# A hybrid layer on one core: the state-space stage with its last convolution tap in the projection's bank, its step size as one fp32r product, and its jobs in another order

## The chip, the cores and the metric

The kernel runs on one core of a Trainium2 chip. The core has a matrix engine (TensorE, PE in the profile; its weight loads are shown apart as PEld), a vector engine (VectorE, DVE), a scalar engine (ScalarE, ACT), a programmable engine (GpSimd, POOL), and a queue engine (SyncE, SP) that issues the transfers. Each engine runs its own instruction list in order, and they wait for one another through semaphores. SBUF is the on-chip memory, PSUM the eight banks into which PE writes. The metric is the device time of one execution in microseconds (us); less is better.

## The reference

The input is x with shape (16, 512, 256): 16 rows of 512 tokens with 256 channels, in fp32. Four residual layers follow one another, each on a layer norm: a state-space layer, a mixture of 8 experts, causal attention, and the same mixture again. Only the first one is touched here:

```python
xz = x @ in_proj_w + in_proj_b
xc, z = jnp.split(xz, 2, axis=-1)                 # 512 channels each
xc = silu(causal depthwise conv of 4 taps over the tokens (xc) + conv_b)
dBu = xc @ x_proj_w + x_proj_b
delta_s, B, u = jnp.split(dBu, [16, 32], axis=-1) # 16, 16, 512 wide
delta = softplus(delta_s @ dt_proj_w + dt_proj_b)
A = -jnp.arange(1, 17)
h[t] = exp(delta[t] * A) * h[t-1] + delta[t] * B[t] * u[t]   # 512 x 16 states
y = h.sum(-1) + u * D
y = y * silu(z)
out = x + (y @ out_proj_w + out_proj_b)
```

## The kernel before

The state-space stage is `mamba_phase`, which fills the span from the start to about 1750 us; the experts and the attention follow in phases of their own and are not touched. Channels lie on the 128 partitions (four groups of 128, numbered m or dt), tokens along the free axis (512). A row's 16 states times four groups are worked off as 32 steps (`STEPS`), two states a step. Step s of a row is: ACT makes `exp(-n*delta)` for two states into the PSUM tile `da` (two activations, `decay_step`, L686), POOL multiplies `du` with the broadcast B rows into `dbu` (`input_step`, L599), DVE runs one scan over 1024 elements into `hs` (`scan_step`, L738), and PE adds the two states of all tokens, transposing, into the bank `yT` (`sum_step`, eight transposes, L838).

How far the engines can run apart is set by their buffers. `da` has two, so decay s waits for scan s-2. `dbu` and `hs` have four (`DEEP`), so dbu s waits for scan s-4, and scan s waits for sum s-4 of PE.

Three rows are in flight. A turn of 32 steps runs `main` work of row turn-1 (the steps), `first` work of row turn (norm, projection, convolution, step size), and `late` work of row turn-2 (output projection, residual, routing). There are 18 turns; turns 3 to 14 run in a hardware loop of two turns a pass. What stands where is written by hand: each engine has a `one_turn` with lines of the form `if s == 9 and first:`, and behind each step's own instruction comes what is listed for that s.

The extra work goes through three PSUM banks, `ring`. `RING_JOBS` is the order in which jobs take them; a job's bank is its index modulo 3, and PE waits (`job_bank`) until the job three places before it has been read. `MM_JOBS`, `ACT_JOBS` and `DVE_JOBS` are the orders in which the jobs' semaphores are raised. The jobs are: T0, T1 the transposed row; I0 to I3 and Z0 to Z3 the two halves of the input projection (`in_proj`, L792); S the 16 step-size inputs and the 16 B values (`x_proj_small`, L808); DA0 to DA3 the step size (`dt_proj`, L822); U0 to U3 the inputs u (`x_proj`, L815); G0 to G3 the summed y turned back (`turn_back`, L846); O0, O1 the output projection (`out_proj`, L855 for the bias, L857); RT0, RT1, RL, RP the routing.

The steps of the code that the change touches: 

- The convolution (`conv_input`, `conv_taps`). ACT copies the projection from its bank to `xc` (L621), and writes the last tap, scaled and with its bias, to `last_tap` (L624). PE overwrites the bank with three shifted products with diagonal matrices (L800), and adds `last_tap` with a fourth product with the identity (L801).
- The step size. ACT adds the bias and writes S to `db`, 48 partitions (`delta_b`, L656). PE multiplies `db[0:32]` with `w_dt` in fp32 (L822). SP stores `db[32:48]` to memory, from where it is spread to all partitions as `bb`. ACT then takes |v| and relu(v) (`step_size`, L660, L661), exp and log (`exp_part`, `log_part`, L666, L670), with a table load on either side of the log, and POOL adds the two parts (`softplus`, L605).
- The output bias, an fp32 product over 32 partitions of which one is used (L855), one for each of four token groups.
- `skip_input` (L676) writes u*D into `uD`, `step_input` (L728) makes `du`, `gate` (L746) makes y*silu(z), `residual` (L751) adds the row, `route_apply` and `prompt_apply` are the norms' four activations (L190).

## Time and profile before

| | us |
|---|---|
| median of 3 runs | 3327.88 (3322.89 to 3331.84) |
| the profiled execution | 3320.98 |
| its span, first to last instruction | 3319.2 |
| state-space stage, about | 0 to 1750 |
| two turns in the loop (678.36 to 893.47) | 215.1 |

The profile comes from one execution. Busy time of an engine counts its computing instructions; the ends of PE's instructions are modelled, so that the distance between the starts of two of them says more than the length of one. An fp32 product of PE leaves two records. "Idle before" is the time in which an engine stood still ahead of an instruction, with what ended the wait.

### The profile page before, as it was taken

To read this page: it belongs to the slowest core of one execution; us is meant where nothing else is said; L and a number is where in the kernel's file an instruction comes from. 1 tells how busy PE (TensorE), PEld (TensorE's weight loads), DVE (VectorE), ACT (ScalarE), POOL (GpSimd) and SP (SyncE) were. 2 spreads that over 40 slices of the span, in tenths; PEclk is the share of its full clock that TensorE was granted. 3 is DMA by queue.
4 is the path that set the end of the run, shared out by engine and by line. 5 is a ranking of instruction groups with operands and counts; after the bars stand their busy time and mean duration, and the time that the engine had idled before them with its cause. 6 is when DMAs were issued, how large, how long until landed. Compare 5 with 4: busy or idle time off the path is not lost. (4 is left out here: it accounts for less than half of the span.)

```text
span 3319.2 us, 54728 instructions
## 1 busy us (share of the span) xinstructions
PE 2964.6 (89%) x17184; PEld 2291.2 (69%) x17184; DVE 2348.4 (71%) x4213; ACT 1764.5 (53%) x3332; POOL 2189.2 (66%) x1403
## 2 busy tenths in 40 slices
PE   6899989989999899899974999999699995999998
PEld 2566555655656556565653999999577774999998
DVE  2888888888888888888883665665466664566564
ACT  3756666566756666566642554544233333444453
POOL 2878887888888888888884555554134434555554
PEclk8999999999999999999986999999899997999999
DMA  4221211121101211121124454452222223445442
GB/s 116 99 98 66 79 69 50 41 80 71 72 24 72 80 64 54 41 79 69 57 98 146 113 127 92 123 120 53 85 83 85 95 79 106 105 112 125 93 124 47
DMA packets 192656, 281.60 MB, mean 85 GB/s; under 512 B 35941, under 2 KB 164618, under 8 KB 184260
## 3 DMA queue, kind: packets, MB, share of 16 engines
q1 hardware_dynamic: 157124, 236.31, 21.3%
q0 software_dynamic: 35328, 42.76, 7.1%
q8 instruction: 105, 1.72, 0.2%
q14 instruction: 99, 0.81, 0.1%
HBM read 197.28 MB, written 94.72 MB: 88 GB/s over the span
## 5 line engine op out<-in xcount | busy, mean ns | idle before, releaser
L599 POOL TENSOR_TENSOR dbu<-du,bb 128x1024 f32<-128x1024 f32 x512 | 1199.9, 2362 | 152.2 <-DVE hs L738 147.4
L738 DVE TENSOR_TENSOR_SCAN hs<-da,dbu 128x1024 f32<-128x1024 f32 x512 | 1150.8, 2279 | 103.4 <-ACT da L686 36.1
L686 ACT ACTIVATE da<-delta 128x512 f32<-128x512 f32 x1024 | 570.1, 595 | 291.8 <-DVE hs L738 277.5
L838 PEld LDWEIGHTS yT<-ident,hs 128*128 128x128 f32 x4096 | 483.4, 146 | 168.3 <-issue 133.6
L838 PE MATMUL yT<-ident,hs 128*128 128x128 f32 x4096 | 540.5, 281 | 22.4 <-DVE hs L738 22.4
L1304 POOL TENSOR_TENSOR ffn_w_lo<-ffn_w,ffn_w_hi 128x512 fp32r<-128x512 f32 x256 | 344.6, 1373 | 170.0 <-ACT ffn_w_hi L1299 165.8
L1350 PE MATMUL ffn_hbank<-ffn_rowsT_hi,ffn_w_hi 128*128 128x320 f32 x1024 | 339.0, 331 | 43.0 <-DVE ffn_hT_lo L1372 40.8
L1384 PE MATMUL ffn_ybank<-ffn_w_hi,ffn_hT_hi 128*128 128x256 f32 x1280 | 364.4, 285 | 0.7 <-DVE ffn_hT_lo L1372 0.7
L1386 PE MATMUL ffn_ybank<-ffn_w_hi,ffn_hT_lo 128*128 128x256 f32 x1280 | 359.3, 281 | 0.0
L1385 PE MATMUL ffn_ybank<-ffn_w_lo,ffn_hT_hi 128*128 128x256 f32 x1280 | 359.0, 280 | 0.0
L1351 PE MATMUL ffn_hbank<-ffn_rowsT_lo,ffn_w_hi 128*128 128x320 f32 x1024 | 318.9, 311 | 0.0
L1352 PE MATMUL ffn_hbank<-ffn_rowsT_hi,ffn_w_lo 128*128 128x320 f32 x1024 | 318.8, 311 | 0.0
L1370 DVE TENSOR_SCALAR ffn_hbank<-ffn_hbank,ffn_b 128x320 f32<-128x320 f32 x512 | 281.8, 550 | 48.0 <-ACT ffn_hT_hi L1361 46.7
L1361 ACT ACTIVATE ffn_hT_hi<-ffn_hbank,ffn_b 128x320 fp32r<-128x320 f32 x512 | 263.1, 526 | 89.6 <-PE ffn_hbank L1352 87.5
L1401 DVE SCALAR_TENSOR_TENSOR ffn_y<-ffn_b,ffn_part,ffn_y 128x256 f32<-128x256 f32 x160 | 77.6, 485 | 312.7 <-ACT ffn_y L1395 312.7
L387 POOL DMA_INDIRECT slots<-a_r_xn,a_r_send x128 | 128.4, 1003 | 246.7 <-DVE a_r_send L377 211.1
L792 PE MATMUL ring<-xnT,w_in 128*128 128x512 f32 x512 | 252.8, 629 | 27.5 <-ACT uD L676 23.9
L1395 ACT ACTIVATE ffn_y<-ffn_ybank,ffn_part 128x256 f32<-128x256 f32 x160 | 76.0, 475 | 358.7 <-PE ffn_ybank L1386 185.2
L1372 DVE TENSOR_TENSOR ffn_hT_lo<-ffn_hbank,ffn_hT_hi 128x320 fp32r<-128x320 f32 x512 | 251.6, 491 | 17.6
L815 PE MATMUL ring<-hx,w_x 128*128 128x512 f32 x512 | 251.1, 626 | 1.2 <-ACT delta L661 1.2
L1384 PEld LDWEIGHTS ffn_ybank<-ffn_w_hi,ffn_hT_hi 128*128 128x128 f32 x1280 | 241.5, 189 | 1.1 <-DVE ffn_hT_lo L1372 1.1
L1385 PEld LDWEIGHTS ffn_ybank<-ffn_w_lo,ffn_hT_hi 128*128 128x128 f32 x1280 | 241.6, 189 | 0.0
(233 smaller groups left out, 5349.0 us busy)
## 6 DMA issues: line engine op xcount, KB each, us to landing
bb<-b_rows SPq DMA_DIRECT2D x64, 1024.0 KB, 4.5
ffn_w<-L_ffn_W SPq DMA_DIRECT2D x64, 1024.0 KB, 10.1
slots<-empty SPq DMA_DIRECT2D x40, 530.0 KB, 7.2
ffn_rows<-slots SPq DMA_DIRECT2D x32, 662.5 KB, 5.0
a_x<-x_after_mamba SPq DMA_DIRECT2D x32, 512.0 KB
xt<-L_attn_a_x SPq DMA_DIRECT2D x16, 512.0 KB
x<-L_attn_a_x SPq DMA_DIRECT2D x16, 512.0 KB, 4.0
x_after_mamba<-x SPq DMA_DIRECT2D x16, 512.0 KB, 3.0
```

Of the source, the lines that this page charges most:

```text
L599: pool.tensor_tensor(dbu[:, s % DEEP], du[:, dt, :].unsqueeze(1).to_broadcast([P, SN, T]), bb[:, q * SN:(q + 1) * SN, :], ALU.mult).then_i ...
L686: ins = act.activation(da[:, s % 2, i, :], delta[:, par, dt, :], ACT.Exp, scale=-float(q * SN + i + 1))
L738: dve.tensor_tensor_scan(flat[0], flat[1], flat[2], 0.0, ALU.mult, ALU.add).then_inc(scanned.sem, 1)
L838: mm = pe.matmul(yT[:, j * P:(j + 1) * P], hs[:, s % DEEP, i, j * P:(j + 1) * P], k.ident[:], start=False, stop=(q == QS - 1 and i == SN - ...
L1304: pool.tensor_tensor(low, full, high.bitcast(F32), ALU.subtract).then_inc(w_lo.sem, 1)
L1350: pe.matmul(hbank[:, job % 4, 0:HW], w1_hi[:, par, c, ws], rowsT_hi[:, c, rs], start=(c == 0), stop=False)
L1351: pe.matmul(hbank[:, job % 4, 0:HW], w1_hi[:, par, c, ws], rowsT_lo[:, c, rs], start=False, stop=False)
L1352: mm = pe.matmul(hbank[:, job % 4, 0:HW], w1_lo[:, par, c, ws], rowsT_hi[:, c, rs], start=False, stop=(c == NC - 1))
L1370: dve.tensor_scalar(bank, bank, b1[:, par, m:m + 1], 0.0, ALU.add, ALU.max).then_inc(h_full.sem, 1)
L1384: pe.matmul(bank, hT_hi[:, m, rs], w2_hi[:, par, m, :], start=(m == 0), stop=False)
L1385: pe.matmul(bank, hT_hi[:, m, rs], w2_lo[:, par, m, :], start=False, stop=False)
L1386: mm = pe.matmul(bank, hT_lo[:, m, rs], w2_hi[:, par, m, :], start=False, stop=(m == NH - 1))
```

## The change

Three pieces of arithmetic and one of order.

1. **Last tap.** ACT writes the scaled last tap back into the projection's own bank, and the three diagonal products add to it. `last_tap` and the identity product are gone.
2. **Step size.** `w_x` carries the 16 step-size columns three times, so that S has 112 rows: three copies and B. ACT writes 96 rows as fp32r (rounded) to `db` and the B rows to a tile of their own, `b_turn`; DVE replaces the middle copy by its rounding error (`delta_low`). `w_dt` holds rounded weights, rounded weights, and the weights' rounding error. One fp32r product over 96 partitions is then high*high + low*high + high*low. S is raised by DVE now, no longer by ACT, and `store_b` follows the second of ACT's two writes.
3. **Output bias** as three bf16 parts on three partitions, one bf16 product. The parts of weights and bias are made once, by DVE in turns 0 and 1 (`stage_weights`, `stage_bias`), from `x1` as a scratch tile; SP loads 21 instead of 11 constants.
4. **Order.** Jobs and the engines' lines are moved.

```diff
-XW = DI + 48
+XW = DI + 112
...
-RING_JOBS = ("G3", "Z0", "O0", "U2", "T0", "T1", "U3", "I0", "I1", "G0", "O1", "Z1", "I2", "I3", "RT0", "S", "DA0",
-             "DA1", "RT1", "DA2", "DA3", "G1", "RL", "U0", "Z2", "U1", "G2", "RP", "Z3", "-")
+RING_JOBS = ("G3", "Z0", "U2", "T0", "T1", "O0", "U3", "I0", "I1", "O1", "G0", "Z1", "I2", "I3", "RT0", "S", "DA0",
+             "DA1", "RT1", "DA2", "G1", "DA3", "U0", "RL", "Z2", "U1", "G2", "RP", "Z3", "-")
...
             act.activation(xc[:, m, DC - 1:], bank, ACT.Identity, bias=b_in[:, m:m + 1])
-            if has_first(turn - 1) or m >= 2:
-                act.wait_ge(conv_mm.sem, conv_mm.at(turn, m - 1))
-            act.activation(last_tap[:, m % 2, :], bank, ACT.Identity, bias=b_tap[:, m:m + 1],
+            act.activation(bank, bank, ACT.Identity, bias=b_tap[:, m:m + 1],
                            scale=w_conv[:, m, DC - 1:DC]).then_inc(conv_in.sem, 1)
...
-            act.activation(db[:], bank_of("S")[0:48, :], ACT.Identity, bias=b_db[:]).then_inc(act_took.sem, 1)
+            act.activation(db[0:96, :], bank_of("S")[0:96, :], ACT.Identity, bias=b_db[0:96, :]).then_inc(s_split.sem, 1)
+            act.activation(b_turn[96:112, :], bank_of("S")[96:112, :], ACT.Identity,
+                           bias=b_db[96:112, :]).then_inc(s_split.sem, 1)
...
+        def delta_low(dve, turn):
+
+            dve.wait_ge(s_split.sem, s_split.at(turn, 2))
+            dve.scalar_tensor_tensor(db[32:64, :], bank_of("S")[32:64, :], b_db[32:64, :], db[32:64, :].bitcast(F32),
+                                     ALU.add, ALU.subtract).then_inc(dve_took.sem, 1)
...
             for tap in range(DC - 1):
-                pe.matmul(bank, w_diag[:, m, tap, :], xc[:, m, tap:tap + T], start=(tap == 0), stop=False)
-            mm = pe.matmul(bank, k.ident[:], last_tap[:, m % 2, :], start=False, stop=True)
+                mm = pe.matmul(bank, w_diag[:, m, tap, :], xc[:, m, tap:tap + T], start=False,
+                               stop=(tap == DC - 2), skip_group_check=True)
...
-            pe.matmul(bank, w_dt[:, m * P:(m + 1) * P], db[0:32, :], start=True, stop=True).then_inc(ring_mm.sem, 1)
+            pe.matmul(bank, w_dt[:, m * P:(m + 1) * P], db[0:96, :], start=True, stop=True).then_inc(ring_mm.sem, 1)
...
+                        if s == 15 and late:
+                            route_apply(act, turn, turn - 2)
...
+                        if s == 20 and first:
+                            delta_low(dve, turn)
```

What moves, at three places. PE, steps 15 to 20 of turn 2: S (L808), uD (L833), the step-size products (L822), G1 (L846), the routing's turn (L865) and score (L873), the sums (L838). Before:

```order
L808 MATMUL ring<-hx,w_x 48x512 x2
L833 MATMUL yT<-ident,uD 128x128 x4
L838 MATMUL yT<-ident,hs 128x128 x8
L822 MATMUL ring<-db,w_dt 128x512
L838 MATMUL yT<-ident,hs 128x128 x8
L822 MATMUL ring<-db,w_dt 128x512
L865 MATMUL ring<-ident,r_xn 128x128 x4
L838 MATMUL yT<-ident,hs 128x128 x8
L822 MATMUL ring<-db,w_dt 128x512 x2
L838 MATMUL yT<-ident,hs 128x128 x24
L846 MATMUL ring<-ident,ysb 128x128 x4
L873 MATMUL ring<-w_router,r_xnT 128x8 x8
```

After (L842, L867, L856, L880, L899, L872 in the same roles):

```order
L842 MATMUL ring<-hx,w_x 112x512 x2
L867 MATMUL yT<-ident,uD 128x128 x4
L872 MATMUL yT<-ident,hs 128x128 x8
L856 MATMUL ring<-db,w_dt 128x512
L872 MATMUL yT<-ident,hs 128x128 x8
L856 MATMUL ring<-db,w_dt 128x512
L899 MATMUL ring<-ident,r_xn 128x128 x4
L872 MATMUL yT<-ident,hs 128x128 x8
L856 MATMUL ring<-db,w_dt 128x512
L872 MATMUL yT<-ident,hs 128x128 x8
L880 MATMUL ring<-ident,ysb 128x128 x4
L872 MATMUL yT<-ident,hs 128x128 x8
```

The fourth step-size product went from step 18 to step 20, behind G1, and the routing's score from step 21 to step 22, behind the first half of U0.

ACT, the end of turn 2 and the start of turn 3: decays (L686), `skip_input` (L676), `gate_input` (L648, L649), the copy of yT (L695). Before:

```order
L686 ACTIVATE da<-delta 128x512 [waits scanned]
L686 ACTIVATE da<-delta 128x512
L686 ACTIVATE da<-delta 128x512 [waits scanned]
L686 ACTIVATE da<-delta 128x512
L676 ACTIVATE uD<-ring,b_skip,d_skip 128x512 [waits summed,du_ready]
L686 ACTIVATE da<-delta 128x512 [waits scanned,reset_ready]
L686 ACTIVATE da<-delta 128x512
L648 ACTIVATE th<-ring,b_z 128x512 [waits dve_took,ring_mm]
L649 ACTIVATE ring<-ring,b_z 128x512
L695 ACTIVATE ysb<-yT 128x512 [waits ring_mm,summed]
```

After (L695, L685, L190 for the next row's norm, L704 for the copy):

```order
L695 ACTIVATE da<-delta 128x512 [waits scanned]
L695 ACTIVATE da<-delta 128x512
L685 ACTIVATE uD<-ring,b_skip,d_skip 128x512 [waits summed,du_ready]
L190 ACTIVATE xt<-xt,norm_shift,norm_rstd 128x256 [waits norm_rstd_ready]
L190 ACTIVATE xt<-xt,norm_shift,norm_rstd 128x256 x3
L695 ACTIVATE da<-delta 128x512 [waits scanned,reset_ready]
L695 ACTIVATE da<-delta 128x512
L704 ACTIVATE ysb<-yT 128x512 [waits ring_mm,summed]
```

The four activations of the next row's norm stood behind step 26 and stand now between the last `skip_input` and the first decay of the next row; the copy of yT stands ahead of `gate_input`.

DVE, steps 17 to 23 of turn 2: scans (L738), `silu_x` (L715), `gate` (L746), the read of the score (L760). Before:

```order
L738 SCALAR_TENSOR_TENSOR hs<-da,dbu 128x1024 [waits summed,dbu_ready,da_ready]
L715 SCALAR_TENSOR_TENSOR hx<-th,ring 128x512 [waits ring_mm,th_ready]
L738 SCALAR_TENSOR_TENSOR hs<-da,dbu 128x1024 [waits summed,dbu_ready,da_ready] x6
L746 TENSOR_TENSOR y<-ring,sz 128x512 [waits dve_took,ring_mm]
L760 COPY r_logits<-ring 128x32 [waits ring_mm]
```

After (L772, L724, `delta_low` L735, L780, L794):

```order
L772 SCALAR_TENSOR_TENSOR hs<-da,dbu 128x1024 [waits summed,dbu_ready,da_ready]
L724 SCALAR_TENSOR_TENSOR hx<-th,ring 128x512 [waits ring_mm,th_ready]
L772 SCALAR_TENSOR_TENSOR hs<-da,dbu 128x1024 [waits summed,dbu_ready,da_ready] x3
L735 SCALAR_TENSOR_TENSOR db<-ring,b_db,db 32x512 [waits s_split]
L772 SCALAR_TENSOR_TENSOR hs<-da,dbu 128x1024 [waits summed,dbu_ready,da_ready] x3
L780 TENSOR_TENSOR y<-ring,sz 128x512 [waits dve_took,ring_mm]
L794 COPY r_logits<-ring 128x32 [waits ring_mm]
```

`delta_low` stands behind scan 20. PE's first step-size product waits for it, and in PE's list that product stands behind sum 16 and ahead of sum 17. Besides, in each turn: on PE U2 now stands ahead of the output projection, whose four parts moved from steps 0, 1, 10, 10 to 2, 4, 8, 9, and the halves of U1 moved from 24 and 27 to 27 and 29; the bank of RL is now the one that G1 leaves, freed by DVE's `gate` 1 behind scan 23 (before, it was the one of DA2, freed by ACT); on POOL the softplus adds moved by one or two steps and the eight sends (L387) one step ahead; on ACT `route_apply` moved from step 17 to 15, `skip_input` 2 from step 4 to 2, and `gate_input` 2 from 28 to 25.

## Rows read from the trace of the kernel before

**Rows 1.** Busy time in two windows: length, each engine, PE clock, DMA share, GB/s.
```profile
602.00:712.00 110.00, 100.59 (x498) 65.89 (x498) 91.29 (x105) 70.96 (x123) 95.55 (x52) 0.97 0.17 63
688.00:690.00 2.00, 2.00 (x10) 2.00 (x11) 1.73 (x1) 2.00 (x4) 2.00 (x3) 0.50 0.77 319
```

**Rows 2.** ACT's timeline, `log_part` of three turns: start us, us, line, operation.
```profile
678.36 1.91 ACT L670 ACTIVATE xc<-xc 128x2048 f32<-128x2048 f32 x1
...
788.11 1.91 ACT L670 ACTIVATE xc<-xc 128x2048 f32<-128x2048 f32 x1
...
893.47 1.91 ACT L670 ACTIVATE xc<-xc 128x2048 f32<-128x2048 f32 x1
```

**Rows 3.** Waits of PE from 600 to 1200 us: total us, times, longest.
```profile
PE yT L833 <- ACT ysb L695: 28.2, 11, 3.9
```

**Rows 4.** Groups by line, PE, 600 to 1200 us: count, busy us, mean ns, idle.
```profile
L801 PE MATMUL ring<-last_tap,ident 128*128 128x512 f32 x48 | 24.5, 592 | 0.0
L822 PE MATMUL ring<-db,w_dt 32*128 32x512 f32 x40 | 21.1, 626 | 0.0
...
L855 PE MATMUL ring<-b_out,one_row 32*128 32x256 f32 x48 | 16.7, 426 | 0.0
```

**Rows 5.** PE's timeline in the attention, products of fp32r parts (record prints f32).
```profile
2399.80 0.39 PE L1760 MATMUL a_ring<-a_xnT_lo,a_wq_hi 128*128 128x512 f32 x1
2400.02 0.39 PE L1761 MATMUL a_ring<-a_xnT_hi,a_wq_lo 128*128 128x512 f32 x1
```

**Rows 6.** PE's timeline: two restarts after waits, the end of I3.
```profile
687.98 1.12 PE L833 MATMUL yT<-ident,uD 128*128 128x128 f32 x4 [3.86 <-ACT ysb L695]
...
759.26 1.04 PE L838 MATMUL yT<-ident,hs 128*128 128x128 f32 x8
...
1721.68 1.09 PE L865 MATMUL ring<-ident,r_xn 128*128 128x128 f32 x4 [7.09 <-ACT r_xn L190]
1722.56 3.21 PE L838 MATMUL yT<-ident,hs 128*128 128x128 f32 x16
...
1726.94 1.91 PE L838 MATMUL yT<-ident,hs 128*128 128x128 f32 x16
```

**Rows 7.** DVE's timeline over one turn, with the next turn's start (idle before, releaser).
```profile
690.93 2.29 DVE L738 TENSOR_TENSOR_SCAN hs<-da,dbu 128x1024 f32<-128x1024 f32 x1 [1.20 <-PE yT L838]
...
700.28 0.73 DVE L728 SCALAR_TENSOR_TENSOR du<-ring,b_u,delta 128x512 f32<-128x512 f32 x1
...
707.05 2.29 DVE L738 TENSOR_TENSOR_SCAN hs<-da,dbu 128x1024 f32<-128x1024 f32 x1 [3.27 <-issue]
...
762.93 2.28 DVE L738 TENSOR_TENSOR_SCAN hs<-da,dbu 128x1024 f32<-128x1024 f32 x1
...
767.87 2.29 DVE L738 TENSOR_TENSOR_SCAN hs<-da,dbu 128x1024 f32<-128x1024 f32 x1
...
775.67 6.87 DVE L738 TENSOR_TENSOR_SCAN hs<-da,dbu 128x1024 f32<-128x1024 f32 x3 [0.55 <-PE yT L838]
783.18 2.29 DVE L738 TENSOR_TENSOR_SCAN hs<-da,dbu 128x1024 f32<-128x1024 f32 x1 [0.64 <-POOL dbu L599]
...
786.95 0.19 DVE L760 COPY r_logits<-ring 128x32 f32<-128x32 f32 x1 [0.90 <-PE ring L873]
...
789.18 2.29 DVE L738 TENSOR_TENSOR_SCAN hs<-da,dbu 128x1024 f32<-128x1024 f32 x1
...
811.43 0.72 DVE L728 SCALAR_TENSOR_TENSOR du<-ring,b_u,delta 128x512 f32<-128x512 f32 x1
...
815.07 2.29 DVE L738 TENSOR_TENSOR_SCAN hs<-da,dbu 128x1024 f32<-128x1024 f32 x1
```

**Rows 8.** ACT's timeline: the operations whose place or number the change touches.
```profile
684.34 2.06 ACT L190 ACTIVATE xt<-xt,norm_shift,norm_rstd 128x256 f32<-128x256 f32 x4
...
703.71 1.12 ACT L686 ACTIVATE da<-delta 128x512 f32<-128x512 f32 x2 [1.89 <-issue]
...
758.33 0.77 ACT L624 ACTIVATE last_tap<-ring,b_tap,w_conv 128x512 f32<-128x512 f32 x1
```

More of the change, by code:

```diff
@@ L996, in one_turn @@
                             conv_input(act, turn, 0)
[L997 removed]
+                        if s == 10 and main:
                             summed_copy(act, turn, row, 0)
[L999 to L1001 removed]
                             skip_input(act, turn, row, 3)
@@ L1004, in one_turn @@
                             tanh_x(act, turn, 0)
+                            conv_input(act, turn, 1)
                         if s == 13 and first:
@@ L1020, in one_turn @@
                             summed_copy(act, turn, row, 1)
-                        if s == 19 and late:
-                            route_turned(act, turn, 0)
                         if s == 19 and is_turn(turn, 0):
@@ L1079, in one_turn @@
                             silu_z(dve, turn, 3)
+                        if s == 0 and is_turn(turn, 1):
+                            stage_bias(dve)
+                        if s == 1 and late:
                             gate(dve, turn, 3)
```

183 lines of the change are left out of this document (105 added, 78 removed).

## The prediction

> **What bounds the kernel now.** I read the busy time of whole turns first, then who waits for whom, and last the timelines of PE, DVE and ACT over one turn. The change touches only the state-space stage, and there a full turn (110 us in that window) has 100.6 us of PE, 91.3 of DVE, 95.6 of POOL and 71.0 of ACT [rows 1]. So PE looks like the bound, with DVE close behind. The turns' length comes from the log of each turn: 678.36 to 788.11 is 109.75 us, to 893.47 another 105.36 [rows 2], 215.1 for the two turns of a loop pass, 107.55 on average. The longer one is the one with the loop's jump.
>
> PE does stand still: in 600 us it waits 28.2 us for ACT's copy of yT [rows 3], which is the wait at the head of step 24 (3.86 us) and at the turn's start. From the first sum of a row until step 24 it shows no wait at all. So a turn is a chain of pieces with different owners. I cut it in five and price each:
>
> (a) From the end of scan 0 to the end of I3, PE is saturated: scan 0 starts at 707.05 and lasts 2.29, I3 is done when the next row starts at 759.26: 49.9 us [rows 6, 7].
> (b) From I3's end to scan 16 at 762.93: 3.7 us, owned by ACT (two convolution inputs, decays) [rows 6, 7].
> (c) Scan 16 to scan 24, 762.93 to 789.18: 26.3 us, DVE nearly full; its waits are 0.55 for a sum, 0.64 for POOL, 0.90 for the score [rows 7].
> (d) Scan 24 to the end of scan 31 (which is where `step_input` starts, 811.43): 22.2 us [rows 7]. A turn earlier 20.9 (700.28 against a scan 24 at 679.41, one period of 109.8 before).
> (e) To the start of the next scan 0: 3.64 us in one turn (811.43 to 815.07), 6.77 in the one with the jump (700.28 to 707.05) [rows 7].
>
> **The change, part by part.**
>
> PE's work. The identity products: 48 records in 24.5 us are 0.51 each [rows 4], two to a product, four products: 4.1 us a turn gone. The step size: 40 records in 21.1 us, 0.53 each, 4.2 us for eight records; an fp32r product of 512 columns is one record and starts 0.22 us before the next one in the attention (2399.80 to 2400.02) [rows 4, 5], so 0.9 is left and 3.3 go. The bias: 48 records in 16.7 us, 0.35 each, 2.8 us a turn [rows 4]; one bf16 product of 256 columns isn't priced here, between nothing and the 0.22 of an fp32r product twice as wide; I take 0.12, so 2.3 us go. Together 9.7 of PE's 100.6 us. That isn't the gain, since only (a) belongs to PE.
>
> (a) It holds all four bias products (-2.3) and two of the four identity products (-2.0). The writes of ACT that start the two convolutions have the slack to hide, about 0.4 us, followed step by step. The other edits only swap places inside the stretch. Between -4.3 and, if `conv_input` 1, now behind `skip_input` 3 and `tanh_x` 0, comes late, -2.5. I take -3.8.
>
> (b) ACT now has conv 2, decay 15, conv 3 and then `route_apply` (four activations, 2.06 us as its twin in [rows 8]) ahead of decay 16. Conv 3 is two writes, at most 0.77 each and 1.3 together with their overlap; the decay is 1.12 [rows 8]: 1.3 + 2.0 + 1.1 = 4.4 against 3.7, +0.7. The write into PSUM instead of SBUF is priced at the same 0.77 [rows 8]; a bank write could be 0.1 off either way.
>
> (c) Three things are new. DVE does `delta_low`, 32 partitions by 512, like its other operations over 512 elements, `step_input` at 0.73 with its overlap [rows 7]: +0.6. It stands behind scan 20, and PE's first step-size product waits for it with sum 17 queued behind; scan 21 needs sum 17. So after `delta_low` DVE waits for the product (0.22), the sum (0.87) and the handoffs, 1.4 us, where it had waited 0.55 at scan 20 [rows 7]: +0.85. ACT's second write of S is like its other writes of 512 columns, at most 0.77 [rows 8], ahead of decay 21, and hidden by that wait. The score's bank is freed by `gate` 1, after which come the score's 1.7 us: DVE waits 1.9 instead of 0.90 [rows 7], +1.0. Sum +2.5. And PE, now early, stands about 4 us before that first product. After a wait of 3.86 us the next four transposes took 1.12 us at 687.98, and the granted clock from 688 to 690 was 0.50, the lower of its two levels (1.2 instead of 2.4 GHz) [rows 1, 6]. Then sum 17 takes 1.75 instead of 0.87: +0.9. I take +3.4; without new waits it would be +0.6, with both doubled +5.
>
> (d) U1 is moved out of the way of sums 24 and 25. DVE's wait there was 1.20 us at 690.93 [rows 7], and in the next turn it came twice. What is left is eight scans of 2.19, `step_input` 0.9 and a gate's 0.6, 19.1 us against 20.9 and 22.2: -2.5 on average. PE again starts at the lower clock behind its wait for yT, 5 us now; sum 24 then ends 0.1 us ahead of need.
>
> (e) The four activations of `prompt_apply` (2.06 us [rows 8]) now stand before decay 0. DVE's route work hid ACT's `skip_input` and decay before (decay 0 ends at 704.8, with the jump's 1.89 ahead of it [rows 8]); now decay 0 comes 1.0 us late in the turn without the jump and is still hidden in the one with it, where DVE itself is away 3.3 us [rows 7]: +0.5 on average.
>
> Sum: -3.8 + 0.7 + 3.4 - 2.5 + 0.5 = **-1.7 us a turn**. `skip_input` 2, now ahead of decay 3 with its wait for `du` 2, makes scan 3 wait about 1.7 us; PE is behind DVE there, so it costs nothing as long as (a) is PE's.
>
> Turns 2 to 15 have all of this: 14 x 1.7 = 24 us. Turn 0 is serial and loses two of its identity products from the path but gains the split, about -2; turn 1 gets DVE's six small operations of the bias split behind scan 0, +2; turns 16 and 17 have cheaper bias products, -2. In all **-26 us**. SP's ten more constants queue behind the others while PE still works on the first row's projection, and are wanted only at its step 13; of POOL's queue only the softplus adds and sends shift, inside its waits. Experts and attention don't move. Against its own time, 3320.98 (span 3319.2), that is 3295; the runs' median is 6.9 higher, so **3302 us**.
>
> **A rule weighed against the trace.** While nothing but transposes ran behind a wait of 7.09 us, 16 of them took 3.21 us from 1722.56, and the same 16 took 1.91 from 1726.94 [rows 6]: the upper level was granted again without any other product in between. The Trainium skill, "TensorE: Matmul & The Clock Gate", Part 4 (PE-mode transpose), says the reverse, that the full clock doesn't engage for transposes. The trace disagrees, so I don't let the lower level last through steps 17 to 22, where after the change hardly anything but transposes stands. By the page, sums 17 to 22 would all cost 1.75; that is the rival on the slow side.
>
> **Rivals.**
> 1. *The new waits of (c) don't arise*, because ACT and DVE reach step 20 earlier than I think or PE later. For it: PE was saturated right up to that product. Against: by (a) PE is 4 us early. Then (c) costs +0.6 and a turn gains 4.5: 14 x 4.5 + 2 = 65, 3263 us. If all 9.7 us of PE counted, 3190, but DVE's 91.3 forbid most of it.
> 2. *No change.* (d) gives nothing since PE, restarted at the lower clock behind a longer wait, brings sum 24 and U1 as late as before: 2.5 less, net +0.8 a turn; with a little more from (a) it is zero. 3328 us.
> 3. *Slower: the lower clock persists* from the first step-size product to U0. Six sums of 1.75, four products of 0.45, and RT1 and G1 at 0.87 each are 14 us, then U0's half (up to 3.4) and the score; scan 24 comes up to 8 us later than in my sum. It is slower once this costs 1.7 beyond my 0.9, that is if the lower level lasts two or three more sums. At half that, 4 us more than in the sum: 14 x (4 - 1.7) - 2 = 30, 3358 us. For: the wait is there if (a) is right, and almost nothing but short products follows it. Against: the rows at 1722 and 1726.
> 4. *The change doesn't do what it says*: the fp32r product is as dear as fp32. Then PE has 3.3 us more in (c), beside DVE's work: 0.3 to 1 us a turn, inside the forecast's range.
>
> **How the numbers follow.** The forecast (with rival 4) 0.38, 3270 to 3318; rival 1 0.22, 3225 to 3270; no change 0.20, 3318 to 3338; slower 0.20, 3338 to 3390. 0.3% (10 us) is about what a measurement of this kernel can tell from nothing. Range 3240 to 3358: it leaves 0.1 above (rival 3 beyond its middle) and less than 0.1 below; faster 0.60, same 0.20, slower 0.20.
>
> **What would show it.** PE: no wait from scan 0's end to I3 and that stretch near 46 us; a wait of about 4 us ahead of the first step-size product, released by DVE's `delta_low`; a clock of 0.5 behind it. DVE: a new wait at scan 21 for yT of 1.4 to 2.3 us, 1.9 for the score, none at scans 28 and 30. Period of a pair of turns near 211.7. If PE shows no wait at the step size, rival 1 is right; if sums of 1.75 go on past step 18, rival 3. Wrong altogether: a stall at scans 12 to 16 beyond 2 us, from ACT's fuller queue.

## The result and the profile after

The changed kernel takes 3337.69 us (median of 13 runs, 3332.68 to 3344.77), the kernel before 3329.51 (13 runs, 3322.89 to 3335.45) beside it: ratio 1.003, 95% interval 1.0022 to 1.0039. It is 8 us slower, 0.3%, and the interval lies above 1. The profiled execution has a span of 3330.9 us against 3319.2. The forecast was 3302: the time is 36 us above it, and on the other side of the kernel before.

The first view is the busy time of the window that answers to the first line of [rows 1]: length, PE, weight loads, DVE, ACT, POOL, PE clock, DMA share, GB/s. Then the row of the page with each engine's busy time over the span.

```profile
602.00:712.00 110.00, 93.32 (x483) 64.53 (x480) 95.51 (x120) 72.44 (x125) 91.98 (x49) 0.95 0.18 65
```

```profile
PE 2845.7 (85%) x16928; PEld 2290.8 (69%) x16928; DVE 2371.5 (71%) x4237; ACT 1774.6 (53%) x3348; POOL 2186.2 (66%) x1408
```

PE's work did go: 118.9 us less than the 2964.6 before, 7.4 a turn, where the prediction's sum had 9.7. By line, from 600 to 1200 us (count, busy us, mean ns, idle before), against [rows 4]:

```profile
L834 PE MATMUL ring<-xc,w_diag 128*128 128x512 f32 x144 | 66.1, 594 | 0.0
...
L856 PE MATMUL ring<-db,w_dt 96*128 96x512 f32 x20 | 12.2, 612 | 18.7 <-DVE db L735 18.7
...
L889 PE MATMUL ring<-b_out,one_row 96*128 96x256 bf16 x24 | 6.6, 275 | 4.6 <-ACT uD L685 4.6
```

The identity products (24.5 us) are gone, the step size has 20 records in place of 40, the bias 24 in place of 48. By busy time a step-size product keeps 0.61 us and a bias product 0.28 (the prediction had 0.22 and 0.12 from start to start). But the line of the step size now has 18.7 us of idle time in five turns, released by DVE's `delta_low` (L735). It had none.

`log_part` on ACT, as in [rows 2] (start us, us):

```profile
687.66 1.91 ACT L679 ACTIVATE xc<-xc 128x2048 f32<-128x2048 f32 x1
...
796.51 1.91 ACT L679 ACTIVATE xc<-xc 128x2048 f32<-128x2048 f32 x1
...
902.66 1.91 ACT L679 ACTIVATE xc<-xc 128x2048 f32<-128x2048 f32 x1
```

Two turns take 215.0 us; they took 215.1. So the loop neither gained nor lost, and the rest is outside it. Between the two spans there are 11.7 us: `log_part` of turn 0 is 1.8 us later (between this kernel, e7_act_moves and e8_read_later, which are the same up to there, it differs by 1.7 us), turn 1 is 5.6 longer (91.3 from `log_part` to `log_part`, 85.7 before), the fourteen turns after it 1.1 together, the stretch from the last `log_part` to the last scan 2.4, and what follows the last scan, experts and attention above all, 0.8 (it differs by up to 15 us between the traces of all these kernels, though none changes the phases there). Only turn 1 stands clear of that.

DVE's timeline over a turn, as in [rows 7]:

```profile
768.29 2.29 DVE L772 TENSOR_TENSOR_SCAN hs<-da,dbu 128x1024 f32<-128x1024 f32 x1 [1.37 <-ACT da L695]
...
776.23 6.64 DVE L772 TENSOR_TENSOR_SCAN hs<-da,dbu 128x1024 f32<-128x1024 f32 x3
782.91 0.74 DVE L735 SCALAR_TENSOR_TENSOR db<-ring,b_db,db 32x512 fp32r<-32x512 f32 x1
785.25 2.29 DVE L772 TENSOR_TENSOR_SCAN hs<-da,dbu 128x1024 f32<-128x1024 f32 x1 [1.60 <-PE yT L872]
788.24 2.29 DVE L772 TENSOR_TENSOR_SCAN hs<-da,dbu 128x1024 f32<-128x1024 f32 x1 [0.70 <-PE yT L872]
...
796.11 0.19 DVE L794 COPY r_logits<-ring 128x32 f32<-128x32 f32 x1 [2.08 <-PE ring L907]
...
798.32 2.29 DVE L772 TENSOR_TENSOR_SCAN hs<-da,dbu 128x1024 f32<-128x1024 f32 x1
```

And the same time on PE, from the projection's second half to the third step-size product, then ACT's two copies of S:

```profile
776.37 1.97 PE L842 MATMUL ring<-hx,w_x 128*112 128x512 f32 x4 [2.23 <-DVE hx L724]
...
778.61 1.04 PE L872 MATMUL yT<-ident,hs 128*128 128x128 f32 x8
783.70 0.50 PE L856 MATMUL ring<-db,w_dt 96*128 96x512 f32 x1 [4.06 <-DVE db L735]
784.04 1.07 PE L872 MATMUL yT<-ident,hs 128*128 128x128 f32 x8
...
786.19 1.92 PE L872 MATMUL yT<-ident,hs 128*128 128x128 f32 x8
787.76 0.74 PE L856 MATMUL ring<-db,w_dt 96*128 96x512 f32 x1
```

```profile
779.61 0.67 ACT L663 ACTIVATE db<-ring,b_db 96x512 fp32r<-96x512 f32 x1
780.30 0.68 ACT L664 ACTIVATE b_turn<-ring,b_db 16x512 f32<-16x512 f32 x1
```

The waits that the prediction named are all there: 4.06 us ahead of the first step-size product, 1.60 at scan 21, 2.08 for the score, and a sum at the lower clock, though it is sum 18 (1.92 us; granted clock 0.50 from 785 to 788) and not sum 17 (1.07 us). The five stretches, in us, in two turns that follow each other (the first one has the loop's jump ahead of it), and the difference of the means over the loop's turns 5 to 12 (from the scans' starts and the end of I3 in each trace):

| Stretch | before | after | difference | over eight turns | forecast |
|---|---|---|---|---|---|
| (a) end of scan 0 to end of I3 | 50.1, 47.4 | 45.9, 44.6 | -4.2, -2.8 | -3.9 | -3.8 |
| (b) to scan 16 | 3.5, 3.5 | 5.0, 5.0 | +1.5, +1.5 | +1.45 | +0.7 |
| (c) to scan 24 | 26.3, 26.2 | 30.0, 30.6 | +3.8, +4.4 | +4.4 | +3.4 |
| (d) to the end of scan 31 | 22.3, 21.0 | 19.1, 19.1 | -3.2, -1.8 | -2.5 | -2.5 |
| (e) to the next scan 0 | 3.6, 6.4 | 4.5, 6.4 | +1.0, 0 | +0.6 | +0.5 |

With scan 0 itself, 2.3 us a turn, the two turns are 214.9 us on both sides. Cutting at scan 24 turned out to hide the cause, so here is a second cut, along the work that leads to the next row's first `du`: the projection S, the step-size products, `log_part`, the softplus add on POOL, `step_input` 0. Means of eight turns of the loop, worked out from each trace, in us. The experiments stand in it too; they follow.

| Kernel | scan 16 to end of S | to first product | to `log_part` | to `du` 0 | turn |
|---|---|---|---|---|---|
| before | 11.1 | 1.4 | 12.7 | 3.5 | 107.5 |
| after | 10.6 | **5.1** | 13.2 | 4.0 | 107.5 |
| e1_arith (old order) | 9.9 | 5.4 | 12.7 | 5.1 | 108.4 |
| e3_no_low | 10.9 | 2.0 | 12.5 | 4.0 | 104.1 |
| e5_dt_behind | 10.6 | 5.2 | 11.5 | 4.5 | 106.6 |
| e6_split_early | 11.0 | 2.6 | 12.7 | 4.0 | 104.7 |
| e7_act_moves | 10.4 | 5.4 | 13.5 | 4.0 | 107.1 |
| e8_read_later | 10.7 | 5.1 | 13.9 | 3.5 | 107.5 |
| v2_all | 8.4 | 3.0 | 12.3 | **9.1** | 106.4 |
| v5_final | 10.4 | 3.2 | 12.6 | 4.0 | 104.1 |

One column moved by more than 0.6 us: from the end of S to the first product, 1.4 to 5.1 us. The four columns together are 28.6 us before and 32.9 after. The rest of the turn, from `du` 0 to the next scan 16, went the other way, from 78.9 to 74.7: what the change gained there (4.2) it lost on the chain (4.2). No run shows a reason why the two are equal. With the chain at 29.4 to 33.1 us in the changed kernel, e3_no_low, e5_dt_behind, e6_split_early and e8_read_later, that rest stays at 74.4 to 74.7, so in these the turn follows the chain.

### The profile page after: what moved, and what is told of

The parts are those of the page before. It is cut to its first block and busy times, and to the rows that moved or that the text cites. A ratio compares the mean times of both kernels' runs of the same rounds, so it can differ in the third digit from the quotient of the medians.

```text
span 3330.9 us, 54315 instructions
## 1 busy us (share of the span) xinstructions
PE 2845.7 (85%) x16928; PEld 2290.8 (69%) x16928; DVE 2371.5 (71%) x4237; ACT 1774.6 (53%) x3348; POOL 2186.2 (66%) x1408
## 5 line engine op out<-in xcount | busy, mean ns | idle before, releaser
L772 DVE TENSOR_TENSOR_SCAN hs<-da,dbu 128x1024 f32<-128x1024 f32 x512 | 1150.0, 2279 | 150.5 <-ACT da L695 78.0
L695 ACT ACTIVATE da<-delta 128x512 f32<-128x512 f32 x1024 | 570.2, 595 | 222.7 <-DVE hs L772 219.7
L872 PEld LDWEIGHTS yT<-ident,hs 128*128 128x128 f32 x4096 | 516.7, 152 | 117.3 <-issue 68.2
L872 PE MATMUL yT<-ident,hs 128*128 128x128 f32 x4096 | 565.5, 290 | 34.4 <-DVE hs L772 34.4
L1405 ACT ACTIVATE ffn_hT_hi<-ffn_hbank,ffn_b 128x320 fp32r<-128x320 f32 x512 | 263.1, 526 | 89.9 <-PE ffn_hbank L1396 88.2
L387 POOL DMA_INDIRECT slots<-a_r_xn,a_r_send x128 | 128.2, 1001 | 248.1 <-DVE a_r_send L377 212.5
L849 PE MATMUL ring<-hx,w_x 128*128 128x512 f32 x512 | 243.3, 604 | 7.2 <-ACT uD L685 4.0
L1394 PEld LDWEIGHTS ffn_hbank<-ffn_rowsT_hi,ffn_w_hi 128*128 128x128 f32 x1024 | 194.6, 190 | 68.2 <-DVE ffn_hT_lo L1416 48.1
```

Source lines behind the costliest of these rows:

```text
L695: ins = act.activation(da[:, s % 2, i, :], delta[:, par, dt, :], ACT.Exp, scale=-float(q * SN + i + 1))
L772: dve.tensor_tensor_scan(flat[0], flat[1], flat[2], 0.0, ALU.mult, ALU.add).then_inc(scanned.sem, 1)
L872: mm = pe.matmul(yT[:, j * P:(j + 1) * P], hs[:, s % DEEP, i, j * P:(j + 1) * P], k.ident[:], start=False, stop=(q == QS - 1 and i == SN - ...
L1394: pe.matmul(hbank[:, job % 4, 0:HW], w1_hi[:, par, c, ws], rowsT_hi[:, c, rs], start=(c == 0), stop=False)
```

## The experiments

### Arithmetic alone, order alone, and the bias staging

e1_arith has the new arithmetic and the tables and steps of the kernel before, with S moved into DVE's list:

```diff
-RING_JOBS = (..., "DA2", "G1", "DA3", "U0", "RL", "Z2", "U1", ...)
+RING_JOBS = (..., "DA2", "DA3", "G1", "RL", "U0", "Z2", "U1", ...)
```

> The changed kernel's arithmetic (last tap in the bank, three stacked parts, bf16 bias) with the job order of the kernel before; the new middle copy stands at its new place between scans 20 and 21. Theory A, the new order's side effects (conv 3 and the route's normalization ahead of decay step 16, the router's bank behind gate 1, U1 behind skip input 0 in turn 0) ate the gain: stretch (b) near 3.7 us per turn as before, the router wait under 1 us, scan 0 of turn 1 near 76 us, and the time some 20 us under the changed kernel, about 3318. Theory B, the middle copy and the wait of the first step-size product ate it whatever the order: stretch (c) near 30 us per turn, and the time that of the changed kernel, 3335 to 3345.

It took 3344.74 us, ratio to before 1.0053 (1.0036 to 1.007). The changed kernel's interval ends at 1.0039, so e1_arith is no faster and probably slower; its turn is 108.4 us against 107.5. Stretch (b) is nearer its old size (4.0 and 4.3), (c) is 29.2 to 29.4 and the wait for the middle copy 20.3 us in five turns. Theory A falls: the old order doesn't bring the gain back. B holds.

e2_order is the other half, the old arithmetic (`last_tap`, fp32 step size, one copy of S) in the new order.

> The kernel before's arithmetic in the changed kernel's job order. Theory A (order's side effects): the extra idle of turns 0 and 1 without the bias staging is 2 to 4 us, (b) is over 5 us, the router wait over 1.5 us per turn, and the time is above the kernel before's, 3340 to 3360. Theory B (middle copy and its wait): without the middle copy stretch (c) falls to 26 to 27 us per turn, so the time is at or below the kernel before's, 3300 to 3330.

3406.85 us, ratio 1.0236 (1.0218 to 1.0254), above the ranges of both theories. PE waits 54.4 us for ACT's `ysb` from 600 to 1200 us (31.5 in the changed kernel), DVE 16.0 for the score, up to 3.2 at a time. So the new order costs much with the old arithmetic, and costs nothing with the new one. The two can't be priced apart and added, and this run doesn't show what costs in the changed kernel, since so much else is late in it.

e4_stage moves `stage_bias` from turn 1, between scans 0 and 1, to turn 0 behind `delta_low`:

```diff
-                        if s == 0 and is_turn(turn, 1):
-                            stage_bias(dve)
...
+                        if s == 21 and is_turn(turn, 0):
+                            stage_bias(dve)
```

> The changed kernel with the six bias-staging instructions moved from turn 1 (between scans 0 and 1) to turn 0, behind the middle copy, where VectorE is idle. If the 4.3 us they took there were on the path, turn 1 ends about 4 us sooner and the time falls by 4 us, to about 3333.5; if turn 1's other waits cover them, under 1.5 us.

3336.33 us (10 runs), ratio to before 1.0027 (1.0014 to 1.0041): by the ratios 1 us better than the changed kernel, less than the intervals can tell. In the traces `log_part` of turn 1 follows that of turn 0 after 90.5 us, against 91.3 (before 85.7). So the six instructions, 4.3 us long, cost about 0.8. From scan 0 of turn 1 on that is 0.8 too, and there the changed kernel and e8_read_later, which have the same instructions in turns 0 and 1, differ by 0.3; over the whole of turn 1 these two differ by 1.7.

### The middle copy

e3_no_low leaves `delta_low` out, so that its step size isn't the reference's, and ACT's second write raises S:

```diff
-                        if s == 20 and first:
-                            delta_low(dve, turn)
...
                            bias=b_db[96:112, :]).then_inc(s_split.sem, 1)
+            act.wait_ge(s_split.sem, s_split.at(turn, 2))
+            act.sem_inc(act_took.sem, 1)
```

> The changed kernel without the middle copy: its 32 rows keep the high part, so the product of low part and weights is computed from the high part once more and the step size is not the reference's. Prices the middle copy, PE's wait for it ahead of the first step-size product and what follows from that wait. Theory B: PE's wait falls from 4.06 to near 3 us, VectorE's 0.74 us goes, and the waits of scans 21 to 23 shrink by 1.5 to 3 us: (c) 30.3 to 27 to 28 us per turn, time 3290 to 3315. Theory A: most of (c) is the two copies on ACT and the router wait, (c) falls by 0.6 to 1 us only, time 3322 to 3332.

3287.81 us, ratio 0.9882 (0.9865 to 0.9898), 40 us faster than the kernel before and 50 faster than the changed one. A turn takes 104.1 us in place of 107.5, so a 0.74 us instruction is worth 3.4 us a turn. The score's wait is still 2.0 us in it. Theory B, with more behind it than it had claimed: (c) is 27.2, and PE's wait ahead of the first product, expected near 3 us, is gone.

### What about the middle copy costs: its place in time or what is queued behind it

e5_dt_behind puts the first product behind sum 17, e6_split_early has ACT's copies at step 19 and `delta_low` between scans 19 and 20.

```diff
-                        if s == 16 and first:
+                        if s == 17 and first:
                             dt_proj(pe, turn, 0)
-                        if s == 17 and first:
                             dt_proj(pe, turn, 1)
```

> The changed kernel with the first step-size product behind sum 17 instead of ahead of it; nothing else moves. Theory A, the stall comes from what is queued behind the waiting product (sum 17, and behind it scan 21): scan 21 no longer waits for TensorE (1.60 and 2.69 us in the two turns of a pair), the stretch from scan 16 to scan 24 falls by 1 to 2.5 us per turn, log_part's period from 107.5 to about 105.5 to 106.5 us, the time to 3305 to 3325. Theory B, the stall comes from the late middle copy itself (step sizes, then decay steps 22 and 23 behind them on ACT): scan 21's wait turns into an equal one for a decay step and the time stays at 3333 to 3340.

```diff
-                        if s == 20 and first:
+                        if s == 19 and first:
                             delta_b(act, turn)
...
-                        if s == 20 and first:
+                        if s == 19 and first:
                             delta_low(dve, turn)
```

> The changed kernel with both parts of the split one step earlier: ACT's two copies behind decay step 19 and the ysb copy (ahead of decay step 20), VectorE's middle copy between scans 19 and 20. Theory B (late middle copy): TensorE's wait ahead of the first step-size product falls from 4.06 to about 1.8 us, all of the step sizes come 2 us sooner, scan 20 is 0.7 to 1 us later, and stretch (c) falls by 1.5 to 3 us per turn, time 3290 to 3315. Theory A (the place in TensorE's queue decides): the wait is shorter, so the stall behind it is as well, but decay step 20 behind two copies gives back 1 us: (c) falls by 0.5 to 1.5 us, time 3313 to 3330.

One run each, with the kernel before at 3334.89 us beside them: 3318.93 and 3294.88. The kernel before lay between 3320 and 3341 us in its runs on record, so a single time says little below 10 us; the turns of the trace say more. A turn is 106.6 and 104.7 us. Both theories get a part. The queue behind the product is worth 0.9 us a turn: the product is as late as ever (5.2 us behind S), but sum 17 and with it the scans run on. The lateness of the copy is worth 2.8. ACT, DVE and PE in e6_split_early, all within 3 us:

```profile
759.99 0.68 ACT L663 ACTIVATE db<-ring,b_db 96x512 fp32r<-96x512 f32 x1 [2.76 <-PE ring L842]
...
760.70 0.68 ACT L664 ACTIVATE b_turn<-ring,b_db 16x512 f32<-16x512 f32 x1
...
761.41 0.74 DVE L735 SCALAR_TENSOR_TENSOR db<-ring,b_db,db 32x512 fp32r<-32x512 f32 x1 [0.89 <-ACT b_turn L664]
...
762.21 0.50 PE L856 MATMUL ring<-db,w_dt 96*128 96x512 f32 x1 [1.04 <-DVE db L735]
762.55 1.04 PE L872 MATMUL yT<-ident,hs 128*128 128x128 f32 x8
762.55 2.29 DVE L772 TENSOR_TENSOR_SCAN hs<-da,dbu 128x1024 f32<-128x1024 f32 x1 [0.40 <-ACT da L695]
```

In the changed kernel ACT had both copies ready at 780.98, and DVE, in the middle of three scans in a row, took the third part up at 782.91. Here DVE has ended its scan 0.89 us before the copies are ready and takes them at once, and PE waits 1.04 us instead of 4.06. Scan 20 pays 0.40 for it. No run has the second copy alone taken away; e3_no_low still has it, with 2.0 us from S to the product against 1.4 before, so on this path it is worth about the 0.6 between them.

e10_before_early asks whether the kernel before had the same fault: its one copy (L656) goes to step 19.

```diff
-                        if s == 20 and first:
+                        if s == 19 and first:
                             delta_b(act, turn)
```

> The kernel before with its one copy of the step-size inputs (L656) one step earlier on ACT, behind decay step 19; nothing of the change is in it. If the handoff of that copy bounded the kernel before as well, the time falls by 15 to 40 us, 3290 to 3315, and the early split of the changed kernel mends an old fault. If it is the middle copy's handoff that binds, the kernel before doesn't gain: 3322 to 3345.

3333.32 us, ratio 1.0012 (0.9997 to 1.0026): nothing gained. Its first product comes 1.4 us behind S, as in the kernel before: the single copy wasn't held up in ACT's queue. The fault is the changed kernel's own.

### The waits that the prediction priced in (b), (c) and (e)

e8_read_later takes the score's wait off scan 24:

```diff
-                        if s == 23 and late:
+                        if s == 24 and late:
                             route_read(dve, turn, turn - 2)
```

> The changed kernel with VectorE's reading of the router's scores behind scan 24 instead of ahead of it. If the 2.08 us wait is on the path, scan 24 starts about 4 us sooner and the 2.2 us of choosing stand behind it: about 2 us less per turn, 3305 to 3315. If the end of the turn is set by the step sizes (log_part, softplus on GpSimd), step input 0 waits instead and the time stays within 3330 to 3340.

3336.26 us (before 3334.89 beside it), and a turn is 107.5 us, as in the changed kernel. Scan 24 comes sooner, (c) is 27.7 and 26.5, but (d) is 23.1 in place of 19.1. Its timeline where the changed kernel had waited:

```profile
902.42 0.17 DVE L794 COPY r_logits<-ring 128x32 f32<-128x32 f32 x1
...
902.79 1.91 ACT L679 ACTIVATE xc<-xc 128x2048 f32<-128x2048 f32 x1
...
904.77 1.27 POOL L614 TENSOR_TENSOR delta<-delta,xc 128x512 f32<-128x512 f32 x1 [4.85 <-ACT xc L679]
906.25 0.75 DVE L762 SCALAR_TENSOR_TENSOR du<-ring,b_u,delta 128x512 f32<-128x512 f32 x1 [1.65 <-POOL delta L614]
```

`log_part` starts at 902.79, where it started at 902.66. `step_input` 0 needs it by way of POOL, and now waits 1.65 us itself. The score's wait was cover, worth nothing (one run, and a turn of the same length).

e7_act_moves shifts three jobs on ACT: `route_apply` to step 16, `skip_input` 2 to step 3, `prompt_apply` to step 30.

```diff
+                        if s == 3 and main:
                             skip_input(act, turn, row, 2)
...
-                        if s == 15 and late:
+                        if s == 16 and late:
                             route_apply(act, turn, turn - 2)
...
+                        if s == 30 and has_first(turn + 1):
+                            prompt_apply(act, norm, xt, xt, turn + 1)
                         if s == 31 and first:
                             skip_input(act, turn, turn, 1)
-                        if s == 31 and has_first(turn + 1):
-                            prompt_apply(act, norm, xt, xt, turn + 1)
```

> The changed kernel with three ACT jobs moved by one step, in three different stretches, each to test one wait of a scan for its decay step: the route's normalization behind decay step 16 (scan 16's 1.37 us wait should vanish in both turns: stretch (b) from 5.1 to 3.7 us); skip input 2 behind decay step 3 (scan 3's 1.73 us should vanish: (a) shorter by up to 1.7 us, if TensorE isn't the bound there, in which case (a) stays at 46 to 48 us); the prompt's normalization at step 30, in ACT's idle time ahead of skip input 1 (scan 0's 3.14 and 1.11 us shrink to under 1 us: (e) shorter by 1 to 2 us). Sum if all three count, 3 to 4.5 us per turn, 3270 to 3290; if only (b) and (e) do, 3290 to 3305; if TensorE gives it all back, 3325 to 3340.

3329.93 us (before 3334.89 beside it), 0.4 us a turn. Scan 16 no longer waits and (b) is 3.5 and 4.7. Over eight turns (b) gives 0.85 us and (e) 0.4, but (a) grows by 0.45 and (c) by 0.35 and take most of it back. Turn 1 shows more: `log_part` to `log_part` 88.2 us against 91.3, so 3.2 of that turn's 5.6 us go. Scan 0 waits 3.15 us for its decay in place of 5.11, which is the prompt's normalization gone from ahead of it; the rest may be `skip_input` 2, for which scan 3 waited 1.73 (not tried alone).

### Towards a better kernel

The projection's second half waits 2.23 us for `silu_x` 3, behind the next row's statistics on DVE. e9_stats moves these behind scan 23, to where the score's wait is. v1_all_dt and v2_all add the early split, ACT's moves and the staging in turn 0, v1_all_dt the product behind sum 17 as well.

> The changed kernel with VectorE's statistics of the next row (2.36 us behind silu_x 2) moved from between scans 16 and 17 to between scan 23 and the reading of the router's scores, where it waits 2.08 us anyway. If the chain silu_x 3, small projection, split, step-size products, log_part sets the turn, all of it comes up to 2.2 us sooner (TensorE's 2.23 us wait ahead of the projection's second half goes) and the time is 3300 to 3315. If it is not that chain but the place of the middle copy behind scan 20, scan 20 still ends when TensorE lets it, and the time stays at 3325 to 3340.

> The changed kernel with the early split, the three ACT moves, the bias staging in turn 0, the statistics behind scan 23 and the first step-size product behind sum 17. The gains are on one chain and should add in part: the early split gave 42 us, statistics up to 30 us more, ACT moves 5 to 10 us: 3240 to 3270. If TensorE's product stream becomes the limit, 3270 to 3290.

> As the kernel above, with the first step-size product ahead of sum 17 as in the changed kernel. If with the early split the product's wait is gone, its place makes no difference (within 5 us of the kernel above); if the wait is still there, this one is slower by 5 to 15 us.

3377.9, 3313.28 and 3308.38 us (before 3340.8 beside them): the first two lie outside all the ranges expected for them, and the third lies 4.9 us from the second, within the 5 expected. S ends 2 to 3 us sooner in all three, and it doesn't help: `du` 0 comes 9 us after `log_part` instead of 4. DVE in v2_all, the choice of experts behind scan 23, then the same instructions in v5_final (below), with POOL's rows at that time:

```profile
881.31 2.36 POOL L608 TENSOR_TENSOR dbu<-du,bb 128x1024 f32<-128x1024 f32 x1
881.37 2.33 DVE L312 CAST r_whichf<-r_which 128x8 f32<-128x8 uint32 x1
...
883.62 1.27 POOL L614 TENSOR_TENSOR delta<-delta,xc 128x512 f32<-128x512 f32 x1
883.72 1.25 DVE L314 TENSOR_TENSOR r_mask<-iota_e,r_whichf 128x64 f32<-128x64 f32 x1
...
884.85 2.35 POOL L608 TENSOR_TENSOR dbu<-du,bb 128x1024 f32<-128x1024 f32 x1
885.01 2.23 DVE L317 TENSOR_TENSOR r_maskb<-r_mask 128x32 bf16<-128x32 f32 x1
```

```profile
768.92 0.17 DVE L312 CAST r_whichf<-r_which 128x8 f32<-128x8 uint32 x1
769.12 0.22 DVE L314 TENSOR_TENSOR r_mask<-iota_e,r_whichf 128x64 f32<-128x64 f32 x1
769.38 0.19 DVE L317 TENSOR_TENSOR r_maskb<-r_mask 128x32 bf16<-128x32 f32 x1
...
769.75 1.27 POOL L614 TENSOR_TENSOR delta<-delta,xc 128x512 f32<-128x512 f32 x1 [4.13 <-ACT xc L679]
```

Each of the three ends with the POOL instruction beside it: 5.81 us in place of 0.58. The moved statistics made POOL's `prompt_rstd` wait 5.04 us (the change itself had moved it from step 21 to 25, which neither the section on the change nor the prediction names), and its next multiply then ran while DVE chose the experts. In the changed kernel the three take 0.17 to 0.23 us in every turn: POOL stands idle there, waiting for `log_part`.

v3_stats20 and v4_no_act have the statistics behind scan 20, the second one without ACT's moves.

> The changed kernel with the early split, the three ACT moves, the bias staging in turn 0, and the next row's statistics between scans 20 and 21 instead of behind scan 23. Theory P (VectorE's small instructions stretch beside GpSimd's multiply): GpSimd no longer waits for the statistics, its multiply of step 25 is over before the choice of experts starts, the three stretched instructions (2.33, 1.25, 2.23 us) are back at 0.17 to 0.23 us, and scan 24 follows scan 23 within 6 to 7 us instead of 12.3; with silu_x 3 sooner the time is 3240 to 3275. Rival (the order of VectorE's own queue cost it): the stretch stays long and the time is above 3290.

> The kernel above without the three ACT moves: early split, staging in turn 0, statistics between scans 20 and 21. If a turn is bound by the chain from silu_x 3 to log_part and the start of the next turn has slack, the moves are worth under 5 us and this is at 3245 to 3280; if they shorten the path, it is 15 to 40 us slower than the kernel above.

3317.4 and 3317.65 us (before 3323.86). The ranges of the main theories, 3240 to 3275 and 3245 to 3280, failed; the rival's sign for v3_stats20, above 3290 with scan 24 still 10 to 11 us behind scan 23, came, and ACT's moves are worth nothing beside it. POOL no longer waits for the statistics, but scan 21 is 2.5 us later for them. In v4_no_act the scores are read at 887.46, 0.25 us after `log_part` starts (887.21), and the two mask instructions last 1.33 and 2.24 us, now beside POOL's softplus add and the multiply behind it. In the changed kernel the scores are read 0.40 us before `log_part` (796.11 and 796.51), the choice takes 2.2 us, and the softplus add starts 1.99 us behind `log_part`'s start: the choice gets out of the way by 0.2 us.

```profile
798.12 0.19 DVE L317 TENSOR_TENSOR r_maskb<-r_mask 128x32 bf16<-128x32 f32 x1
798.50 1.27 POOL L614 TENSOR_TENSOR delta<-delta,xc 128x512 f32<-128x512 f32 x1 [4.93 <-ACT xc L679]
```

So it is the time beside POOL's work that decides, and both of my places for the statistics lost that margin.

v5_final leaves the statistics where they were and has the rest: early split, the three moves, the staging in turn 0.

> The changed kernel with the early split, the three ACT moves and the bias staging in turn 0; the next row's statistics stay where the changed kernel has them. If only the moved statistics brought the choice of experts beside GpSimd's multiply, its cast and its two mask instructions are at 0.17 to 0.23 us and the gains add: 42 us of the split, some 7 us of the moves: 3280 to 3292, faster than both kernels. If the combination is what shifts it, they are at 1.2 to 2.3 us in many turns and the time is 3300 to 3315.

3285.3 us, ratio to before 0.9865 (0.9848 to 0.9881). It beats both kernels, by 47 us the kernel before beside it (four runs, 3282.92 to 3288.05). Its cast and mask instructions last 0.17 to 0.23 us in all turns, a turn is 104.1 us, and turn 1 is 84.6 us long against 91.3.

## Why the prediction was wrong

The step that failed is the pricing of (c), and with it the sum. The prediction saw the new wait, and its place, but added up only what DVE itself would lose (0.6 + 0.85 + 1.0 + 0.9). It left out that the first step-size product, and behind it `log_part`, the softplus and the next row's `du` 0, come later: 3.7 us from S to that product, which by e3_no_low and e6_split_early is worth 3.4 and 2.8 us a turn. A turn was to gain 1.7 us and gained none: 24 of the 36 us. The rest is mostly in the first and last turns. Turn 1 took 5.6 us more (forecast +2), since ACT's moved norm was not priced there, and the last turns 2.4 us more (forecast -2).

- **What bounds the kernel.** Right for (a) and for PE in it. Wrong in treating (c) as DVE's because DVE was nearly full there (its waits were 0.55, 0.64 and 0.90 [rows 7]). PE was full as well. The busy time of (c), before and after (columns as above):

```profile
762.93:789.18 26.25, 26.25 (x142) 16.57 (x141) 23.48 (x40) 21.93 (x38) 21.85 (x11) 1.00 0.27 87
```

```profile
768.29:798.32 30.03, 23.74 (x137) 17.87 (x136) 24.27 (x39) 21.62 (x35) 18.11 (x10) 0.94 0.23 72
```

  PE had no idle time in it and has 6.3 us of it now, while DVE and ACT have about the work they had. The order in which things become due in (c) and just behind it is S, split, products, `log_part`, softplus, `du` 0, and that chain crosses four engines.
- **(a), -3.8 forecast, -3.5 measured in the two turns, -3.9 over eight.** Right, and its owner too: PE's only wait between its first sum and I3 is 1.55 us ahead of a bias product, in one of the two turns. The bf16 bias product starts 0.11 us before the next one in 54 of 64 cases, where 0.12 was taken.
- **(b), +0.7 forecast, +1.45 measured.** Mis-sized by a start. The sum took conv 3 as beginning with I3's end, told by the next row's start on PE; but ACT was still in conv 2 and decay 15, and conv 3 began at 763.94, 0.77 us after that start (763.17). The rest is as summed: 1.2 for its two writes, 2.0 for `route_apply`, 1.1 for the decay. e7_act_moves shows that it hardly mattered, since without it (a) and (c) took most of the time back.
- **(c), +3.4 forecast, +4.1 measured in the two turns, +4.4 over eight.** The size was 1.0 short, and the make-up wrong. It was priced as four waits of DVE that add: `delta_low` 0.6, scan 21 0.85, the score 1.0, the lower clock 0.9. The score's is worth nothing (e8_read_later). The lower clock is there (0.94 over the stretch against 1.00, and 1.92 us for sum 18), but e6_split_early has the same 0.94 from scan 16 to scan 24 and a turn 2.8 us shorter. In its turn shown above the lower level falls on the second half of S (3.60 us at 756.20, against 1.97 in the changed kernel), so no run gives the clock's own price. What counts is that the first product starts 3.7 us later after S, through ACT's two copies, the scans that DVE was in, and `delta_low`. Taking `delta_low` out gives 3.4 us a turn back (e3_no_low), making it early 2.8 (e6_split_early).
- **(d), -2.5 forecast, -2.5 measured.** Right, and 19.1 us long as summed. The waits that went were at scan 28 (1.20) and, in the longer turn, scan 29 (1.30), not 30.
- **(e), +0.5 forecast, +0.6 over eight turns.** Right, and in the turn forecast: 1.0 us in the one without the jump, nothing in the other.
- **The sum, -1.7 a turn forecast, 0 measured.** Over eight turns (b) cost 0.75 and (c) 1.0 more than forecast, and the rest came out within 0.1. The margin was as thin as these two errors. Besides, the terms don't stand alone. Shortening (b) lengthens (a) and (c) (e7_act_moves), shortening (c) at the score lengthens (d) (e8_read_later): a stretch that ends at a scan is not one that ends on the path.
- **The ends, -2 forecast, +8 in the trace (turn 1 5.6, the last turns 2.4).** Turn 1 was priced at +2 for the six staging instructions. These are worth 0.8 (e4_stage). What cost there were ACT's moves, first of all `prompt_apply`, ahead of decay 0 and the table load where nothing hides it (2.0 of the 3.2 us, e7_act_moves), and the late split (turn 1 is 89.0 us in e6_split_early, 2.3 less). I had looked at `prompt_apply` in the loop only, where DVE's own work covers it. The 2.4 us of the last turns stay open: from the last `log_part` to the last scan it is 120.1 us in the changed kernel, 117.7 before, and 117.1 in e8_read_later.
- **The rivals.** Rival 1 (no new waits) fell at once. Rival 2 (no change) was right on the loop for a wrong reason, since (d) did give 2.5, and its range ends at 3338, 0.3 us above the measured time. Rival 3 (lower clock persists) didn't occur: sum 18 took 1.92 us, and sums 19 and later 1.04. Step-size products stand between these sums. Behind the wait for yT at 805.50 only transposes ran, and the granted clock was 0.50 from 806 to 808 and 1.00 from 809. So the trace again speaks against what the Trainium skill, "TensorE: Matmul & The Clock Gate", Part 4 (PE-mode transpose), says of transposes. Rival 4 didn't occur: at the upper clock an fp32r product starts 0.34 us before the transpose behind it (783.70 to 784.04), where the sum had taken the 0.22 between two fp32r products, and at the lower one 0.57 (787.76 to 788.33). By busy time, fp32's two records took 1.06 [rows 4].

## What to carry to other kernels

When a change puts a small step between two engines, don't price its own 0.7 us or the wait that shows on one queue, but follow the whole hand-over: where in its queue each engine stands when the data come. Here copies that were ready 1.9 us before the end of DVE's scans waited for that end, and one step earlier in both queues made a turn 2.8 us shorter, the kernel some 40 us faster. Cut a loop where a datum is handed on (S, the products, the log), not at a landmark of an engine that has slack, and check each wait you mean to remove for what becomes late next.

## What the runs showed of the hardware

Some of DVE's instructions, small as they are, last as long as POOL's instruction beside them. The cast of 8 elements takes 0.17 us alone and 2.33 beside POOL's multiply; the mask instructions 0.22 and 0.19 against 1.25 and 2.23; a subtraction in the bias staging 0.42 in turn 0 (e4_stage) and 2.56 in turn 1 beside POOL's multiply (the changed kernel). The Trainium skill says why, in "SBUF — State Buffer", section "SBUF: two separate sides": the two engines share a pair of ports that one instruction holds for its whole length, and DVE wants it when it runs in a two-port mode or has two SBUF inputs. The trace agrees for the mask instructions and the subtraction, whose two inputs are both in SBUF; whether the cast, with one input, ran in such a mode can't be seen in it. The scans read `dbu` from SBUF and `da` from PSUM, so they have one SBUF input only, and they don't collide: 163 scans that lie wholly beside POOL's multiplies take 2.28 us on average, 46 with no multiply beside them 2.29, and the multiply is 2.36 beside a scan and 2.35 without one. So before a small instruction of DVE is moved beside POOL's work, look where its inputs lie, and then in the trace.
